# All 32 tiles of the ternary feed-forward written out, with VectorE's and ScalarE's order within a tile changed

## The reference, cut to what matters

```python
x = x + xattn0(ctx, ctx, layernorm(x), ...)          # stage a, 16 heads
x = x + ffn0(layernorm(x), w_gate, w_up, w_down)     # stage b, ternary
x = x + xattn1(layernorm(x), ctx, ...)               # stage c, 8 heads
x = x + routed_ffn(layernorm(x), ...)                # stage m

def act_quant(x):                                    # one scale per row
    scale = 127.0 / clip(max(abs(x), axis=-1), 1e-5)
    return clip(round(x * scale), -128, 127) / scale
def bitlinear(x, w):  return act_quant(x) @ weight_quant(w).T   # w: -1, 0, 1 times a scale
def ffn0(x, w_gate, w_up, w_down):
    return bitlinear(silu(bitlinear(x, w_gate)) * bitlinear(x, w_up), w_down)
```

## Time and profile before

| | |
|---|---|
| median of 3 runs | 2059.81 us |
| the profiled execution's own time | 2061.22 us |
| its span | 2059.5 us |
| TensorE busy over the span | 1955.5 us (95%) |
| VectorE busy | 1325.7 us (64%) |
| ScalarE busy | 1044.1 us (51%) |
| GpSimd busy | 790.7 us (38%) |

### The profile page before, as it was taken

The page is one execution under the profiler, slowest core; times in us unless marked ns, Lnnn a source line. Parts: engine busy times, 40 slices in busy tenths (PEclk is TensorE's granted clock), DMA queues, the critical chain, the costliest instruction groups (busy, mean ns, idle before and its releaser), DMA issues.

```text
span 2059.5 us, 44547 instructions
## 1 busy us (share of the span) xinstructions
PE 1955.5 (95%) x14044; PEld 1484.6 (72%) x14044; DVE 1325.7 (64%) x4065; ACT 1044.1 (51%) x2717; POOL 790.7 (38%) x1437
## 2 busy tenths in 40 slices
PE   5999999999999799999978999999999999999998
PEld 4788888888887444444337888888888876788776
DVE  4777777777776677777764565565555565454475
ACT  3677767667777534445433454444544443222242
POOL 2454545545456544544541212222122213232254
PEclk8999999999999899999998999999999999999999
DMA  6131122113114445576542111212112136222131
GB/s 191 40 132 63 59 80 96 59 59 117 59 57 175 142 115 129 131 177 163 137 97 89 43 42 54 71 41 83 41 52 73 42 113 204 94 102 81 57 128 42
DMA packets 184066, 192.17 MB, mean 93 GB/s; under 512 B 96240, under 2 KB 106480, under 8 KB 183936
## 3 DMA queue, kind: packets, MB, share of 16 engines
q1 hardware_dynamic: 183936, 190.66, 29.7%
HBM read 136.08 MB, written 33.57 MB: 82 GB/s over the span
## 4 chain that ended last, share of the span: by engine, by line
PE 77%; DVE 9%; issue 5%; POOL 3%; ACT 3%; DMA 2%; DVEq 0%; POOLq 0%; SPq 0%; ACTq 0%
PE bank L1007 19%; PE bank L996 17%; PE bank L2472 12%; PE bank L1064 7%; PE bank L1669 6%; PE bank L1077 4%; PE bank L1047 4%; PE bank L1682 2%; PE bank L987 2%; DMA b_xqT<-b_xq 1%; DVE c_probs L786 1%; DVE b_hpart L1577 1%; POOL b_hround L1423 1%; PE bank L2378 1%; DVE c_pT L795 1%
## 5 line engine op out<-in xcount | busy, mean ns | idle before, releaser
L496 POOL TENSOR_SCALAR a_probs<-a_probs,a_rinv 128x256 f32<-128x256 f32 x512 | 237.5, 482 | 283.9 <-DVE a_rinv L802 283.9
L617 ACT ACTIVATE a_probs<-a_probs,a_negm 128x256 f32<-128x256 f32 x512 | 254.6, 502 | 117.0 <-DVE a_negm L786 116.3
L496 POOL TENSOR_SCALAR c_probs<-c_probs,c_rinv 128x256 f32<-128x256 f32 x128 | 67.1, 534 | 396.9 <-DVE c_rinv L802 396.9
L786 DVE CUSTOM_DVE_ANT_0 a_probs<-bank,a_mbias 128x256 f32<-128x256 f32 x512 | 191.7, 417 | 6.3 <-PE bank L1047 4.3
L2472 PE MATMUL bank<-m_xnT,m_s 128*128 128x512 f32 x768 | 187.3, 395 | 2.7 <-DVE m_hid L2213 2.7
L1478 ACT ACTIVATE b_gate<-bank,b_xs 128x512 f32<-128x512 f32 x128 | 87.4, 683 | 197.4 <-PE bank L1669 193.0
L795 DVE COPY a_pT<-bank 128x512 f32<-128x512 f32 x128 | 88.3, 690 | 141.8 <-PE bank L1064 141.7
L617 ACT ACTIVATE c_probs<-c_probs,c_negm 128x256 f32<-128x256 f32 x256 | 127.4, 502 | 90.0 <-DVE c_negm L786 90.0
L2472 PEld LDWEIGHTS bank<-m_xnT,m_s 128*128 128x128 f32 x768 | 144.5, 190 | 34.2 <-DVE m_hid L2213 3.1
L1064 PE MATMUL bank<-a_ident,a_probs 128*128 128x128 f32 x1024 | 155.9, 275 | 13.9 <-POOL a_probs L496 7.0
L1669 PE MATMUL bank<-b_wg,b_xqT 128*128 128x512 bf16 x512 | 133.4, 383 | 12.7 <-DMA b_xqT<-b_xq 12.4
(11 more groups left out here) (279 smaller groups left out, 4420.3 us busy)
## 6 DMA issues: line engine op xcount, KB each, us to landing
m_ew<-in_L_ffn_w_dram SPq DMA_DIRECT2D x24, 512.0 KB, 8.5
a_cbuf<-in_ctx_dram SPq DMA_DIRECT2D x16, 512.0 KB, 5.9
a_xbuf<-in_x_dram SPq DMA_DIRECT2D x16, 512.0 KB, 5.7
a_resb<-in_x_dram SPq DMA_DIRECT2D x16, 512.0 KB, 3.8
x<-a_resb SPq DMA_DIRECT2D x16, 512.0 KB, 2.8
b_xbuf<-x SPq DMA_DIRECT2D x32, 256.0 KB, 2.8
b_resb<-x SPq DMA_DIRECT2D x32, 256.0 KB, 3.0
x<-b_resb SPq DMA_DIRECT2D x32, 256.0 KB, 2.0
```

The costliest lines, as they stand in the source:

```text
L496: last = nc.gpsimd.tensor_scalar(pr, pr, rinv[:, s, r:r + 1], 0.0, ALU.mult, ALU.add)
L617: nc.scalar.activation(pr, pr, ACT.Exp, bias=negm[:, s, h % 2, t:t + 1], scale=-1.0, accum_out=ssum[:, s, QT * (h % 2) + t:QT * (h % 2) + ...
L786: nc.vector.tensor_tensor_reduce(out=probs[:, s, h % 2, t], in0=s_bank[h][:, t * SEQ:(t + 1) * SEQ], in1=mbias[:, el.par], scale=-sm_scale ...
```

## The change

All 32 iterations of stage b are written out. The work beside moves up by ten tiles (loads from tile 4, query bias at tile 8, gain at 9, high parts at 10 to 13), and the low parts are written in quarters of 128x512 at tiles 12 to 27. VectorE takes `x_scale` behind part 0 of `hidden` instead of part 1, and `row_stats` of tile n+3 behind `rows_out` of tile n instead of within `hidden`; the work beside comes behind both. ScalarE takes the first half of `integers_h` before gate parts 0 and 1, and the second half before parts 2 and 3. GpSimd's, TensorE's and SyncE's orders within an iteration stay.

```diff
-        if tile == 14:
+        if tile == 4:
             load_columns(sp)
-        if 14 <= tile < 22:
-            load_weight(sp, MADE[(tile - 14) // 2], (tile - 14) % 2)
+        if 4 <= tile < 12:
+            load_weight(sp, MADE[(tile - 4) // 2], (tile - 4) % 2)
...
-        if tile == 18:
+        if tile == 8:
             query_bias(pe)
...
-        if 21 <= tile < 29:
-            lo_of_weight(dve, MADE[(tile - 21) // 2], (tile - 21) % 2)
+        if 12 <= tile < 28:
+            lo_of_weight(dve, MADE[(tile - 12) // KC], (tile - 12) % KC)
...
+    def each_tile(iteration):
+        for n in range(tiles):
+            iteration(Element(n // 2, n % 2, tiles))
...
         def iteration(el):                      # ScalarE
-            for half in range(HALVES):
-                if el.has(1):
-                    silus(el.plus(1), [half])
-                integers_h(el, half)
+            integers_h(el, 0)
             if el.has(1):
-                silus(el.plus(1), range(HALVES, NC))
+                silus(el.plus(1), [0, 1])
+            integers_h(el, 1)
+            if el.has(1):
+                silus(el.plus(1), range(2, NC))
...
+                if steady and c == 0 and el.has(1):     # VectorE, in hidden
+                    x_scale(dve, el.plus(1))
                 if c > 0:
                     largest(c - 1)
...
-                if steady and c == 1 and el.has(1):
-                    x_scale(dve, el.plus(1))
-                if steady and c == 2 and el.has(2):
-                    row_stats(dve, el.plus(2))
...
         def iteration(el):                      # VectorE
             if el.has(1):
                 hidden(el.plus(1))
-            if beside and number(el):
+            if beside and el.n == tiles - 1:
+                beside.vector_units(dve)
+            rows_out(el)
+            if el.has(3):
+                row_stats(dve, el.plus(3))
+            if beside and el.n:
                 beside.vector_beside(dve, el.n)
-            rows_out(el)
-
-        run_elements(dve, tiles, iteration, ahead=AHEAD)
+
+        each_tile(iteration)
```

More of the change, by code:

```diff
@@ L354, in sync_between @@
     def sync_between(sp, tile):
-        if tile == 14:
+        if tile == 4:
             load_columns(sp)
-        if 14 <= tile < 22:
-            load_weight(sp, MADE[(tile - 14) // 2], (tile - 14) % 2)
-        elif tile == 22:
+        if 4 <= tile < 12:
+            load_weight(sp, MADE[(tile - 4) // 2], (tile - 4) % 2)
+        elif tile == 12:
             load_first(sp, cbuf[0][:], ctx_in, 0, c_loaded)
-        elif tile == 23:
+        elif tile == 13:
             load_masks(sp)
@@ L479, in gpsimd_beside @@
     def gpsimd_beside(pool, tile):
-        if tile == 16:
+        if tile == 6:
             gpsimd_constants(pool)
@@ L589, in scalar_beside @@
     def scalar_beside(act, tile):
-        if tile == 18:
+        if tile == 8:
             bias_column(act)
-        elif tile == 19:
+        elif tile == 9:
             gain_weight(act)
-        elif 20 <= tile < 24:
-            hi_of_weight(act, MADE[tile - 20])
+        elif 10 <= tile < 14:
+            hi_of_weight(act, MADE[tile - 10])
     def scalar_units(act):
@@ L697, in scalar, with lo_of_weight @@
         attn_hi(Element(0, batches - 1, batches), GROUPS - 1)
-    def lo_of_weight(dve, name, half=None):
+    def lo_of_weight(dve, name, piece=None):
         n, _, stage, w = WEIGHTS[name]
         hi, lo = (w[:, part].rearrange("p k n -> p (k n)") for part in (HI, LO))
-        cut = slice(0, KC * DIM) if half is None else slice(half * KC * DIM // 2, (half + 1) * KC * DIM // 2)
+        cut = slice(0, KC * DIM) if piece is None else slice(piece * DIM, (piece + 1) * DIM)
         dve.wait_ge(w_hi, n + 1)
         last = nc.vector.tensor_tensor(lo[:, cut], stage[:, cut], hi[:, cut].bitcast(F32), ALU.subtract)
-        if half == 0:
+        if piece is not None and piece < KC - 1:
             return
@@ L774, in vector_beside, with vector_units @@
             row_stats(dve, Element(0, 0, batches))
-        elif tile == 31:
-            for u in PROLOGUE[:7]:
-                lo_of(dve, Element(0, 0, batches), u)
+    def vector_units(dve):
+        for u in PROLOGUE[:7]:
+            lo_of(dve, Element(0, 0, batches), u)
     def vector(dve, beside=None):
@@ L1128, in attention_phase @@
     phase.scalar_beside, phase.scalar_units, phase.vector_beside = scalar_beside, scalar_units, vector_beside
+    phase.vector_units = vector_units
     phase.tensor_beside, phase.tensor_units = tensor_beside, tensor_units
@@ L1299, in ternary_ffn_phase @@
     made = {"rows": stored}
-    AHEAD = 18
+    def each_tile(iteration):
+        for n in range(tiles):
+            iteration(Element(n // 2, n % 2, tiles))
     def half_of_tile(half):
@@ L1349, in iteration @@
             sp.dma_start(dst, resb[:, el.par]).then_inc(stored[el.par], 16)
-        run_elements(sp, tiles, iteration, ahead=AHEAD)
+        each_tile(iteration)
         if beside:
@@ L1441, in iteration @@
                 round_h(el.plus(1))
-        run_elements(pool, tiles, iteration, ahead=AHEAD)
+        each_tile(iteration)
     def integer(act, n, c):
@@ L1502, in iteration @@
                 beside.scalar_beside(act, el.n)
-        run_elements(act, tiles, iteration, ahead=AHEAD)
+        each_tile(iteration)
     def vector_sums(dve, el, quad):
@@ L1701, in iteration @@
             down(el, beside)
-        run_elements(pe, tiles, iteration, ahead=AHEAD)
+        each_tile(iteration)
     phase = Phase(sync, gpsimd, scalar, vector, tensor, sems)
```

## The result

The kernel after takes 2235.41 us (median of 4 runs, 2229.04 to 2235.94) against 2059.93 us before (median of 4): ratio 1.0851, interval 1.0822 to 1.088. It is slower by 175.5 us; I had forecast 2195, so the direction and the loop of waits were right, but the size was 40 us short and outside the range of 2150 to 2228.

What follows compares the result with a forecast made beforehand. TensorE was taken as the bound, VectorE close behind; after the change a loop of waits would bound each tile. 100.6 + 6 + 5 + 2 + 0 + 22 = 135.6 us on 2059.8 gave 2195 us, range 2150 to 2228.

Steps and rivals of the forecast that it cites:

- The closed loop: Stage b, tiles 0 to 29: statistics behind rows_out delay rounding and hidden; 14.65 us per tile against 11.18, +100.6 us.
- The clock of TensorE: TensorE idling some 4.1 us per tile drops to 1.2 GHz in half the tiles: +22 us, bounds 0 and 46.
- Rival 1: TensorE's clock falls in every tile, costing 46 us: 2220 us in all; chance 0.13.
- Quarters beside GpSimd: Low-part quarters on VectorE slow GpSimd's normalise: 0.4 us in each of 16 tiles, +6 us (0 to 8).
- Query bias: At tile 8, its work on TensorE ahead of down lies on the path: +5 us (4 to 6).
- Start and end: Iteration 0 waits for first integers and x_scale, +2 us (0 to 2.2); tiles 30 and 31, 0 us (-2 to 2).
- The loads for c: Loads at tiles 4 to 11 could delay transposes past their 0.4 us slack: 0 to 8 us, taken as 0.
- What the intended edits could win: Loop's extra and work beside, 0.76 us above TensorE's 10.42 in 29 periods: 22 us at most.

Runs made afterwards that it cites:

- run 3: Kernel after plus twelve products that nobody reads in TensorE's stall, ahead of gate part 2, from tile 2 on: 2178.09 us, ratio 1.0573.
- run 7: Kernel before with only the row statistics of tile n+3 moved behind rows_out of tile n: 2156.4 us, ratio 1.0476.
- run 1: Kernel after with the row statistics taken within hidden again, behind part 2: 2061.4 us, ratio 1.0008.
- run 4: Kernel after with GpSimd's rounding of tile n+1 put ahead of the normalising of tile n+3: 2119.57 us, ratio 1.0293.
- run 10: Kernel after plus four products that nobody reads in TensorE's stall: 2203.11 us, ratio 1.0686.
- run 11: Kernel after plus eight products that nobody reads in TensorE's stall: 2205.83 us, ratio 1.0696.
- run 9: Kernel after with statistics within hidden and ScalarE's order as before; x_scale stays behind part 0: 2043.43 us, ratio 0.9907.
- run 6: Kernel before with all 32 tiles written out and nothing else changed: 2060.97 us, ratio 0.9997.
- run 2: Kernel after with ScalarE's order alone as before (gate part 0, integers, gate part 1, integers): 2165.48 us, ratio 1.0514.
- run 5: Kernel after with the places of x_scale and row_stats and ScalarE's order as before; writing out and quarters kept: 2054.51 us, ratio 0.9972.

## Why the prediction was wrong in size

- **The closed loop: right.** 29 periods without a clock fall behind a stall are 437.1 us in run 3 (734.70 to 1171.83). Without the clock I had 424.9 + 6 + 5 = 435.9. The move of the statistics alone (run 7) and undoing it (run 1) show that it is the cause; GpSimd's place in line (run 4) is a link of it.
- **The clock of TensorE: the step that failed.** I took half of the tiles at 1.6 us, 22 us, with 46 as the bound. The runs show 28 of the 29 stalls with a fall, and 497.6 - 437.1 = 60.5 us, 2.2 each on the average (17.07 less run 3's periods is 2.18 where a quarter stands beside, 2.46 elsewhere). Both factors were low. The price came from places where the clock fell just after the products began again; here it fell 1.3 to 2.7 us before them in 26 of the 28, and TensorE spent three groups at half speed (1.68, 1.71 and 1.59 us instead of 0.87 each, start to start). And the count: each of the 29 periods is 16.1 us or longer, and ten in succession lie between 17.06 and 17.08, so that a fall at the same place of each tile is the steady state and not a matter of chance. The one stall without a fall, of 3.89 us, stands ahead of the query bias; the clock fell behind the bias instead, as it did in the kernel before and in run 3, so that this period is only 0.2 us longer than run 3's. Windows of the kernel after at this place (TensorE alone):

```profile
857.00:861.00 4.00, 0.11 (x2) 1.00 0.23 66
861.00:864.00 3.00, 2.99 (x14) 1.00 0.72 153
869.00:870.00 1.00, 1.00 (x5) 0.63 0.12 45
```

With less of a stall (runs 10 and 11) only part of the tiles had a fall. Rival 1, which I gave 0.13, had the count nearly right and would still have been 15 us short. The Trainium skill (TensorE: Matmul & The Clock Gate, HAM oscillation) says that a wait that is long enough and comes in every pass has the array throttled in every pass; the trace agrees in 28 of 29 stalls. The same section gives a penalty of half the throttled time. By that the 6.8 us at half speed of the tile shown would cost 3.4; they cost 2.4, half of the 4.8 in which there were products.
- **Quarters beside GpSimd: right in kind.** It was 0.28 us a tile (14.89 against 14.61), 4.5 in all, for my 0.4 and 6. GpSimd's first small operation took 0.47 instead of 0.19 us and ended at 1029.86, just behind VectorE's quarter at 1029.81. The Trainium skill (SBUF — State Buffer, Who interferes with whom) says that a VectorE instruction with two SBUF inputs and a GpSimd one that reads SBUF contend for ports under an exclusive lock; the trace agrees. In the kernel after even this cost was gone, since most tiles kept to about 17.1 us with a quarter or without.
- **Query bias:** the period that ends at tile 8 is 20.04 us in run 3 and the next one 14.96, 5.1 for my 5. **Start and end:** +2.4 for my +2, and -1.8 for my 0.
- **The loads for c:** at most the 1.6 us by which three periods of run 3 among these tiles exceed 14.61 (14.96, 15.49 and 14.96), for my 0. Another 1.7 us lies in four later periods (15.21, 15.24, 15.35 and 15.49 against 14.89); no run tells why.
- **What the intended edits could win:** I had put it at 22 us at most, from the periods. The best version (run 9) wins 17, and 11 of them come from the earlier scale, which I had not credited with anything since the loop hid it. The part that I had ascribed to the loop's branches was no gain (run 6).

The sum by what was measured: 2.4 + (437.1 - 324.2) + 60.5 - 1.8 = 174.0 us, the difference of the two spans (2233.5 - 2059.5).

## What to carry to other kernels

When work is moved on one engine, write down for each other engine what stands behind the instruction that waits for it, and add the hops once around: here a move of 0.9 us of statistics behind a wait put the 4.6 us from `rows_out` to the rounding on the path of every tile. When a sum says that TensorE will stand still for some 4 us in each tile, price its clock in every tile and not in a share of them, with all the groups behind the stall that run at half speed (2.2 to 2.5 us here). Test the parts of a change one by one: two of the parts here were gains (6 and 11 us), and the two that were losses hid them.

## What the runs showed that I had not expected

- TensorE's clock fell in about half of the tiles or more with stalls of 2.15 to 2.44 us (16 falls in run 2, 20 in run 11), mostly after the products had begun again, but behind none of run 3's stalls, which were 1.29 to 1.64 us but for one of 1.91 and one of 2.16. Single stalls do not tell the whole: in run 4 the clock fell near 1083.1 behind two short ones in succession, of 0.85 and 0.96 us.
- Periods lock: with the clock falling in each tile, most tiles with and without a quarter beside them were equally long (17.06 to 17.15 us), though 0.28 us apart where the clock stayed up.
- A transposing DMA of 128x512 took 2.5 us in most tiles and 4.1 to 4.3 us in some (runs 5 and 6), with no more than stage b's own transfers and c's loads beside it. What makes the slow ones is open.
